# Adjacency build of a four-layer graph network: cells padded to one chunk of 128 edges in place of two

## The reference

```python
edge_index = jnp.stack([src, dst])
deg = jnp.maximum(jax.ops.segment_sum(jnp.ones(dst.shape, jnp.float32), dst, num_segments=1250), 1.0)
h = jnp.maximum(_layernorm(x, axis=-1), 0.0)
x = x + _L0_gnn_ref(h, src, dst, deg, ...)              # mean of neighbours
h = jnp.maximum(_layernorm(x, axis=-1), 0.0)
x = x + _L1_gnn_ref(h, edge_index, edge_weight, ...)    # two convolutions, weighted, normalised
h = jnp.maximum(_layernorm(x, axis=-1), 0.0)
x = x + _L2_gnn_ref(h, edge_index, edge_attr_128, ...)  # a message per edge, then a GRU
h = jnp.maximum(_layernorm(x, axis=-1), 0.0)
x = x + _L3_gnn_ref(h, edge_weight1, ..., src, dst)     # sum weighted by edge_weight1
```

## Time and profile before

| | |
|---|---|
| median of three runs | 1614.16 us |
| the profiled execution, its own time | 1613.28 us |
| its span | 1611.6 us |
| PE (TensorE) busy | 1336.9 us, 83% |
| DVE (VectorE) busy | 1173.5 us, 73% |
| POOL (GpSimd) busy | 798.6 us, 50% |
| ACT (ScalarE) busy | 620.8 us, 39% |
| mean granted TensorE clock | 0.948 |

### The profile page before, as it was taken

The page is one execution under the profiler, slowest core; times in us unless marked ns, Lnnn a source line. Parts: engine busy times, 40 slices in busy tenths (PEclk is TensorE's granted clock), DMA queues, the critical chain, the costliest instruction groups (busy, mean ns, idle before and its releaser), DMA issues.

```text
span 1611.6 us, 20246 instructions
## 1 busy us (share of the span) xinstructions
PE 1336.9 (83%) x4074; PEld 702.6 (44%) x4074; DVE 1173.5 (73%) x1917; ACT 620.8 (39%) x1580; POOL 798.6 (50%) x859
## 2 busy tenths in 40 slices
PE   0179169279999999896999888899899899999898
PEld 0144124134444444345875444444344444444665
DVE  8999863379999999982258277888888666666532
ACT  0122111066666662013001166777777422222310
POOL 1637777756666664677777256666666200000000
PEclk9989579689999999897999989999999999999999
DMA  8363402210000004444334476666566500000220
GB/s 347 108 263 120 117 22 80 87 32 0 0 0 0 0 0 190 152 134 154 101 92 127 170 223 218 186 186 178 171 187 190 142 0 0 0 0 1 78 86 31
DMA packets 81186, 168.21 MB, mean 104 GB/s; under 512 B 15436, under 2 KB 37838, under 8 KB 77812
## 3 DMA queue, kind: packets, MB, share of 16 engines
q1 hardware_dynamic: 52996, 102.58, 18.3%
q0 software_dynamic: 25472, 59.97, 13.3%
q10 hardware_dynamic: 2672, 5.11, 1.0%
HBM read 116.17 MB, written 51.44 MB: 104 GB/s over the span
## 4 chain that ended last, share of the span: by engine, by line
PE 52%; DVE 13%; DMA 12%; issue 11%; POOL 9%; ACT 2%; DVEq 0%; POOLq 0%; ACTq 0%; SPq 0%
PE pb L922 19%; PE pb L971 17%; POOL cell_rows L601 6%; DMA arena<-p_rows,gidx 5%; PE pb L998 5%; PE pb L1151 4%; DMA arena<-dst_rows 4%; DVE arena L1214 2%; DMA cell_rows<-pay,idx 2%; PE pb L1006 2%; POOL arena L662 2%; PE pb L908 1%; PE pb L1088 1%; DVE arena L1242 1%; DVE arena L1209 1%
## 5 line engine op out<-in xcount | busy, mean ns | idle before, releaser
L662 POOL DMA_INDIRECT arena<-p_rows,gidx x184 | 189.1, 1028 | 103.0 <-POOL gidx L658 72.8
L601 POOL DMA_INDIRECT cell_rows<-pay,idx x168 | 169.4, 1008 | 88.2 <-issue 46.6
L641 POOL DMA_INDIRECT dst_rows<-ering,idx x168 | 173.9, 1035 | 78.0 <-issue 37.1
L1088 PE MATMUL pb<-arena 128*128 128x512 f32 x368 | 197.0, 618 | 4.5 <-ACT arena L807 4.5
L971 PE MATMUL pb<-arena 128*128 128x384 f32 x368 | 141.2, 508 | 44.4 <-POOL arena L617 38.6
L1436 DVE TENSOR_TENSOR arena<-pb,arena 128x512 f32<-128x512 f32 x184 | 126.4, 687 | 66.4 <-DMA arena<-p_rows,gidx 61.0
L703 ACT ACTIVATE arena<-iota,cellm 128x128 f32<-128x128 f32 x368 | 127.7, 394 | 115.4 <-PE pb L971 78.4
L922 PE MATMUL pb<-ws,tiles 128*128 128x512 f32 (+1 forms) x360 | 147.3, 557 | 11.5 <-ACT tiles L674 11.5
L971 PE MATMUL pb<-tiles,arena 128*128 128x384 f32 x368 | 140.0, 504 | 6.0
L813 ACT ACTIVATE high<-arena 128x512 fp32r<-128x512 f32 x184 | 115.5, 627 | 75.6 <-DVE arena L1436 73.9
L1097 PE MATMUL pb<-high,low 128*128 128x512 f32 x184 | 111.4, 606 | 28.1 <-DVE low L1441 26.0
(11 more groups left out here) (205 smaller groups left out, 2227.7 us busy)
## 6 DMA issues: line engine op xcount, KB each, us to landing
dst_rows<-arena SPq DMA_DIRECT2D x6, 2046.0 KB, 18.1
arena<-dst_rows SPq DMA_DIRECT2D x46, 264.0 KB, 3.0
ering<-in_edge_attr_dram SPq DMA_DIRECT2D x41, 256.0 KB, 3.0
arena<-adj SPq DMA_DIRECT2D x10, 640.0 KB, 4.1
arena<-in_x_dram SPq DMA_DIRECT2D x18, 256.0 KB, 4.9
arena<-in_L_gnn_W_hh_dram SPq DMA_DIRECT2D x3, 1024.0 KB, 11.8
wt_hh<-ws SPq DMA_DIRECT2D x3, 1024.0 KB, 7.4
arena<-in_L_gnn_W_ih_dram SPq DMA_DIRECT2D x3, 1024.0 KB, 7.8
```

The source lines that it names most:

```text
L601: nc.gpsimd.indirect_dma_start(cell_rows[:, :], bass.IndirectOffsetOnAxis(idx1[:, c:c + 1], 0), pay1[:, c, :], None).then_inc(c_scattered[ ...
L641: nc.gpsimd.indirect_dma_start(dst_rows[:, :], bass.IndirectOffsetOnAxis(idx2[:, c + k:c + k + 1], 0), ering[:, 4 * q + k, :], None).then_ ...
L662: nc.gpsimd.indirect_dma_start(rows[:, k, :], None, p_rows[:, :], bass.IndirectOffsetOnAxis(gidx[:, k:k + 1], 0)).then_inc(g_landed[k], 16)
L1088: nc.tensor.matmul(e_bank(k)[:], erowT[:, k % 4], w1e_sb, start=True, stop=True).then_inc(edge_mm, 1)
```

## The change

Each cell is rounded up to whole chunks of 128 edges, not to whole pairs. There are then at most 272 chunks (34 turns of 8), and each is a step of its own on TensorE and VectorE: one product with `start` and `stop`, its own bank of the four, its own `block_done`, its own cell read from `cell_at` and its own add. Two adjacent chunks may now belong to different cells. The one-hots and their weights are still made for two chunks in one instruction, 136 times. A turn is now 8 chunks, four comparisons and eight adds, in the order comparison, add, add. The waits on the rings are counted in chunks: the one-hots' ring is as deep as before (8 chunks), the banks' ring now holds four chunks. The table of cells has three columns in `tabf` in place of two, and the destination table moves to the fourth; `cellm` becomes a part of a tile `free`, whose later users stay.

```diff
-CELL_PAIRS = (E + CELLS * (PAIR - 1)) // PAIR
-CELL_PAIRS = -(-CELL_PAIRS // 8) * 8
-CELL_CHUNKS = 2 * CELL_PAIRS
+CELL_CHUNKS = (E + CELLS * (P - 1)) // P
+CELL_CHUNKS = -(-CELL_CHUNKS // 8) * 8
...
-        cellm = sb("cellm", [P, CELL_CHUNKS, 4])
+        free = sb("free", [P, 2 * D + 2 * P])
+        cellm = free[:, 0:CELL_CHUNKS * 4].rearrange("p (c w) -> p c w", c=CELL_CHUNKS)
...
             def weights_turn(i):
-                for q in range(TURN):
-                    pool.wait_ge(dst_hot, TURN * i + q + 1)
+                for q in range(TURN // 2):
+                    pool.wait_ge(dst_hot, TURN // 2 * i + q + 1)
                     passed()
-                    hot = ohd(2 * (q % 4), 2)
+                    hot = ohd(2 * q, 2)
...
             def build_blocks():
                 def turn(i):
-                    for q in range(TURN):
-                        n, place = TURN * i + q, q % 4
-                        at_least(pe, block_added, n - 3)
-                        pe.wait_ge(src_hot, n + 1)
-                        pe.wait_ge(weighted, n + 1)
-                        for k in range(2):
-                            ins = nc.tensor.matmul(pb[place][:, 0:3 * P], ohs[:, 2 * place + k],
-                                                   ohd(2 * place + k, 1).rearrange("p a m d -> p (a m d)"), start=k == 0, stop=k == 1)
-                        ins.then_inc(block_done, 1)
+                    for k in range(TURN):
+                        at_least(pe, block_added, TURN * i + k - 3)
+                        if k % 2 == 0:
+                            pe.wait_ge(src_hot, TURN // 2 * i + k // 2 + 1)
+                            pe.wait_ge(weighted, TURN // 2 * i + k // 2 + 1)
+                        nc.tensor.matmul(pb[k % 4][:, 0:3 * P], ohs[:, k], ohd(k, 1).rearrange("p a m d -> p (a m d)"),
+                                         start=True, stop=True).then_inc(block_done, 1)
...
-            places(B1, cell_b, CELL_CHUNKS, "prefix1", idx1, [0, 1], THIRD, order_ready[0])
+            places(B1, cell_b, CELL_CHUNKS, P, "prefix1", idx1, [0, 1, 2], THIRD, order_ready[0])
...
             def hots(i, q):
 
-                n = TURN * i + q
-                at_least(dve, block_done, n - 3)
-                vtt(ohd(2 * (q % 4), 2)[:, :, 0], iota1[:].unsqueeze(1).to_broadcast([P, 2, P]),
-                    cellm[:, bass.ds(2 * TURN * i + 2 * q, 2), 1:2].to_broadcast([P, 2, P]), ALU.is_equal).then_inc(dst_hot, 1)
-
-            def add_block(i, q):
-
-                n = TURN * i + q
+                at_least(dve, block_done, TURN * i + 2 * q - 6)
+                vtt(ohd(2 * q, 2)[:, :, 0], iota1[:].unsqueeze(1).to_broadcast([P, 2, P]),
+                    cellm[:, bass.ds(TURN * i + 2 * q, 2), 1:2].to_broadcast([P, 2, P]), ALU.is_equal).then_inc(dst_hot, 1)
+
+            def add_block(i, k):
+
+                n = TURN * i + k
                 at = dve.value_load(cell_at[0:1, bass.ds(n, 1)], min_val=0, max_val=(CELLS - 1) * P)
                 dve.wait_ge(block_done, n + 1)
                 at_least(dve, block_added, n)
                 cell = matrices[:, :, bass.ds(at, P)]
-                vtt(cell, pb[q % 4][:, 0:3 * P].rearrange("p (m d) -> p m d", m=3), cell, ALU.add).then_inc(block_added, 1)
+                vtt(cell, pb[k % 4][:, 0:3 * P].rearrange("p (m d) -> p m d", m=3), cell, ALU.add).then_inc(block_added, 1)
 
             def turn(i, last):
-                for q in range(TURN):
-                    if not last or q < TURN - 3:
-                        hots(i + (q + 3) // TURN, (q + 3) % TURN)
-                    add_block(i, q)
+                for q in range(TURN // 2):
+                    if not last or q < TURN // 2 - 3:
+                        hots(i + (q + 3) // 4, (q + 3) % 4)
+                    add_block(i, 2 * q)
+                    add_block(i, 2 * q + 1)
```

More of the change, by code:

```diff
@@ L139, in build_gnn @@
         tabf = sb("tabf", [P, 4])
-        places_at = sb("places_at", [1, CELL_PAIRS + DST_PAIRS], I32)
-        cell_at = places_at[:, 0:CELL_PAIRS]
-        dst_at = places_at[:, CELL_PAIRS:]
+        places_at = sb("places_at", [1, CELL_CHUNKS + DST_PAIRS], I32)
+        cell_at = places_at[:, 0:CELL_CHUNKS]
+        dst_at = places_at[:, CELL_CHUNKS:]
         gidx = sb("gidx", [P, GROUP], I32)
@@ L240, in build_gnn @@
         w1e_sb = adj_part(D)
-        free = cellm[:].rearrange("p c w -> p (c w)")
         hot_far = free[:, 2 * D:2 * D + 2 * P].rearrange("p (c f) -> p c f", c=2)
@@ L453, in _ @@
                 sp.wait_ge(c_scattered[k], 16 * (J // COL))
-            sp.dma_start(cellm[:].rearrange("p c w -> p (c w)"),
+            sp.dma_start(free[:, 0:CELL_CHUNKS * 4],
                          cell_rows.rearrange("(p c) w -> p (c w)", p=P)[:, 0:CELL_CHUNKS * 4]).then_inc(cells_loaded, 16)
@@ L459, in _ @@
                 sp.dma_start(ering[:, 4 * q:4 * q + 4, 0:DE], edge_v[:, 4 * q:4 * q + 4, :]).then_inc(e_loaded[q], 16)
-            sp.wait_ge(block_added, CELL_PAIRS)
+            sp.wait_ge(block_added, CELL_CHUNKS)
             edges3 = [0, NT * D, (NT + 2 * KT) * D, 2 * NT * D, AW]
@@ L699, in turn @@
                 def turn(i):
[L700 to L701 removed]
+                    for q in range(TURN // 2):
+                        at_least(act, block_done, TURN * i + 2 * q - 6)
                         for k in (2 * q, 2 * q + 1):
[L703 to L704 removed]
+                            ins = nc.scalar.activation(ohs[:, k], iota1[:], ACT.Abs,
+                                                       bias=cellm[:, bass.ds(TURN * i + k, 1), 0:1].rearrange("p a w -> p (a w)"))
                         ins.then_inc(src_distance, 1)
[L706 to L707 removed]
+                        act.wait_ge(src_distance, TURN // 2 * i + q + 1)
+                        two = ohs[:, 2 * q:2 * q + 2].rearrange("p c s -> p (c s)")
                         nc.scalar.activation(two, two, ACT.Relu, bias=1.0, scale=-1.0).then_inc(src_hot, 1)
                 turn(0)
[L711 removed]
+                with act.Fori(1, CELL_CHUNKS // TURN) as i:
                     turn(i)
@@ L1017, in degrees @@
                 ins.then_inc(for_act, 1)
-            pe.wait_ge(block_added, CELL_PAIRS)
+            pe.wait_ge(block_added, CELL_CHUNKS)
             pe.wait_ge(z_loaded[0], 16)
@@ L1203, in _, with places @@
             link(vts(pay2[:, :, 1], dt_f, 1.0, -1.0, ALU.add, ALU.mult))
-            def places(buckets, bucket_of, chunks, job, idx, tab_cols, width, ready):
+            def places(buckets, bucket_of, chunks, unit, job, idx, tab_cols, width, ready):
                 ohb, csb = oh[:, 0:buckets], cs[:, 0:buckets]
@@ L1330, in add_block @@
                 cell = matrices[:, :, bass.ds(at, P)]
-                vtt(cell, pb[q % 4][:, 0:3 * P].rearrange("p (m d) -> p m d", m=3), cell, ALU.add).then_inc(block_added, 1)
+                vtt(cell, pb[k % 4][:, 0:3 * P].rearrange("p (m d) -> p m d", m=3), cell, ALU.add).then_inc(block_added, 1)
             def turn(i, last):
-                for q in range(TURN):
-                    if not last or q < TURN - 3:
-                        hots(i + (q + 3) // TURN, (q + 3) % TURN)
-                    add_block(i, q)
+                for q in range(TURN // 2):
+                    if not last or q < TURN // 2 - 3:
+                        hots(i + (q + 3) // 4, (q + 3) % 4)
+                    add_block(i, 2 * q)
+                    add_block(i, 2 * q + 1)
             dve.wait_ge(cells_loaded, 16)
             dve.wait_ge(wt_stored[0], 32)
-            turns = CELL_PAIRS // TURN
+            turns = CELL_CHUNKS // TURN
             for q in range(3):
@@ L1347, in _ @@
             turn(turns - 1, True)
-            dve.wait_ge(block_added, CELL_PAIRS)
+            dve.wait_ge(block_added, CELL_CHUNKS)
             def degree(m, t):
```

35 lines of the change are left out of this document (15 added, 20 removed).

## The result

The changed kernel takes 1637.68 us (median of 4 runs, 1636.04 to 1640.22) against 1613.74 us (4 runs, 1610.86 to 1614.77) on the same chip: a ratio of 1.0153, interval [1.0133, 1.0172]. It is 24 us slower. Its profiled execution took 1638.54 us with a span of 1636.8 us and a mean granted clock of 0.944, against 1613.28, 1611.6 and 0.948. A second comparison, among the experiments, gave 1.0129 [1.0097, 1.0161]. Ratios and their intervals leave out disturbed executions, which are slower at a lower granted clock; the medians of times in the experiments include them.

What follows compares the result with a forecast made beforehand. A comparison-weighting ring (VectorE, GpSimd) bound the build before; VectorE's queue would after: +19.8 (loop) - 1.1 (cell load) = +18.7 us on 1613.3, giving 1632, or 1633 by the median; range 1615 to 1655.

Steps and rivals of the forecast that it cites:

- the queue as the bound: Main forecast, chance 0.80: VectorE's in-order queue, 0.97 us an add, sets the changed build's pace at the high clock.
- Step 1, the ring alone: Build: the cycle comparison, GpSimd weighting, comparison, 1.597 us each, would alone give 217 us for 136 rounds, not 293.
- Step 2: Build: VectorE's queue needs 9.3 us a turn, so the loop ends at 644.1 us, +19.8 us.
- step 5: Before the build: loading fewer cells takes 3.2 us in place of 4.3, -1.1 us.
- Step 3: Build: a pair's second add waits for the first, 0.75 us start to start, covered by the queue's 0.97.
- Step 4: Build: four PSUM banks holding four chunks cost nothing; the comparison falls to 0.42 us without gain.
- VectorE's busy time down by over 100 us: Sign of the main forecast: VectorE's busy time falls by over 100 us while the loop is longer.
- Steps 5 and 6: Before the build: the shorter cell load, -1.1 us; the sort's extra table column, nothing, at most +0.5 us.
- Step 7: Behind the build: all engines wait for the last add and no operation changes, so the shift goes through whole.
- B: Rival, chance 0.08: the comparison and weighting cycle stays the build's bound, 217 us, about 1537 us in all.
- C: Rival, chance 0.07: TensorE's clock falls in the build; +37 us for half the time low, +73 for all.
- D: Rival, chance 0.05: an add costs only 0.85 to 0.91 us of queue; about no change, 1602 to 1617 us.

Runs made afterwards that it cites:

- 2: Changed kernel with the third matrix left out of the build: build 308.8 us, time 1852.63 us, ratio 1.011 to the kernel before.
- 1: Changed kernel with each add sent to a fixed cell, no place loaded in the build: build 216.9 us, time 1772.25 us, ratio 0.967.
- 4: Kernel before with the cell's place loaded twice for each add: build 346.3 us, time 1883.56 us, ratio 1.028.
- 6: Changed kernel without the run-time bounds check on the load of the cell's place: build 248.5 us, time 1785.2 us, ratio 0.980.
- 3: Kernel before with the third matrix left out of the build: build 225.8 us, time 1760.28 us, ratio 0.960.
- 5: Kernel before with each add sent to a fixed cell, no place loaded in the build: build 290.5 us, time 1850.86 against 1822.98 us.
- a_fixed: Same run as 1: changed kernel with adds to fixed cells, no place loaded in the build; 1772.25 us, ratio 0.967.
- a_unchecked: Same run as 6: changed kernel, the place's load without its run-time bounds check; 1785.2 us, ratio 0.980.
- after_again: Changed kernel run once more without an edit, beside the kernel before: 1635.43 us, ratio 1.0129.
- a_turn16: Changed kernel with turns of 16 chunks in place of 8: build 289.3 us, time 1607.9 us in its one run.
- a_unchecked_16: Changed kernel with the place's load unchecked and turns of 16 chunks: build 230.0 us, time 1553.08 us in its one run.
- a_unchecked_16_mid: Changed kernel with unchecked load, turns of 16 chunks and the comparison between a pair's two adds: build 224.5 us, time 1544.19 us, ratio 0.9558.
- a_two_matrices: Same run as 2: changed kernel, third matrix left out of the build; 1852.63 us, ratio 1.011.
- b_two_loads: Same run as 4: kernel before, the cell's place loaded twice for each add; 1883.56 us, ratio 1.028.
- four_per_load: Changed kernel with four chunks' places packed in one integer, loaded once for four adds: build 288.2 us, time 1826.3 us, ratio 1.005.

## Why the prediction was right, point by point

The predicted 1633 us stands against 1637.68, the shift of +18.7 against +23.9. (The loop's part of the sum is 644.1 - 624.4 = 19.7, not 19.8; it changes nothing.) The mechanism of the forecast, the queue as the bound, is shown: by 2 (the engines' work doesn't matter), 1, 4 and 6 (the queue's work does, both ways), 3 and 5 (in the kernel before it was the other way round).

- **Step 1, the ring alone.** 217 us for 136 rounds: a_fixed took 216.9.
- **Step 2, the turn.** 9.3 predicted, 9.23 measured; 32 turns 295.5 us (adds that start at 337.36 and 632.84) in place of 297.6, -2.1. The terms, too: 0.97 an add (three of four steps; the fourth is 0.90), 1.72 over the seam (0.97 + 0.17 + 0.58), and 0.28 in place of 0.25 for the comparisons' extra register operations. The last turn took 6.8 us (6.7), the first ended its last add's start at 337.4, where 339.2 less the earlier start of step 5 gives 338.1.
- **Step 3, the wait.** 0.75 us, hidden below 0.97. Uncovered in a_unchecked, it was 0.76.
- **Step 4, banks and comparison.** Nothing, and a mean of 0.43 us. But the sign "VectorE's busy time down by over 100 us" was too large: 1173.5 to 1082.9, -90.6 us. By the durations the comparisons lose 162 us (184 x 1.20 to 136 x 0.43) and the adds gain 51 (184 x 0.544 to 151.6), -111. But before, each add began inside the end of one comparison (472.07, and 470.94 + 1.21 = 472.15) and ended inside the start of the next, and busy time counts such a stretch once: some 28 us less to lose. After, adds and comparisons overlap by some 9 us. -111 + 28 - 9 = -92, against -90.6 measured: the overlap is what I left out.
- **Steps 5 and 6, the way to the build.** The first comparison came 2.1 us earlier, not 1.1. The load of the cells did take less (3.4 in place of 4.3 us from issue to landing, 0.9); the other 1.2 us are the scatter of the cells, which ended at 322.6 in place of 323.8 us. No reason for that was found in the change.
- **The end of the build.** 640.2 against 643.0: -0.7 by the start, -2.1 by the turns. +15.9 in place of +18.7.
- **Step 7, behind the build, is the step that failed.** "The shift goes through whole" gave 0, and the profiled execution shows +9.3 us. The build ended 2.8 us earlier than predicted, which hides a part of it in the sum; that is luck. From the end of the build to the end of the span it took 987.3 us before, 996.6 after, and 995.4 in after_again, which would fit a cost of the change. But the kernels with the same code and the same padding behind another build took 986.3 (a_turn16), 990.2 (a_unchecked_16) and 991.7 (a_unchecked_16_mid), one execution each, so that code and the padding alone don't bring it. Chance of one execution is unlikely too: the medians of the changed kernel are 24 and 22 us above the kernel before, and the build's end, where the profiles have it, accounts for 16 and 17 of them. One part was found, the low clock at the end of the build: the window of 37 us from there, before, after and in a_turn16 (us, PE busy (x), PEld, DVE, ACT, POOL, granted clock, DMA share, GB/s):

```profile
624.00:661.00 37.00, 36.61 (x100) 17.30 (x100) 36.91 (x18) 0.00 (x0) 12.03 (x16) 1.00 0.80 297
```

```profile
640.00:677.00 37.00, 36.77 (x89) 16.77 (x89) 36.73 (x18) 0.00 (x0) 10.52 (x14) 0.96 0.79 294
```

```profile
619.00:656.00 37.00, 36.19 (x97) 17.05 (x97) 36.71 (x18) 0.00 (x0) 11.16 (x15) 1.00 0.80 298
```

TensorE is as busy in all three, and gets 89 passes done where the others get 100 and 97. Its block of 80 passes takes 36.1 us in the changed kernel and 36.3 in after_again, and 34.6 to 34.7 in the kernel before and in a_turn16. That is 1.4 us on the chain. Most of the rest comes between the first load from `ys`, which starts 36.8 to 38.5 us behind the build in all the kernels compared, and the first gather: that starts 296.0 us behind the build before, 305.2 after, 303.4 in after_again, 301.7 in a_turn16 and 300.7 in a_unchecked_16_mid. In a_turn16 the end of the span doesn't come later for it: its first gather is 5.7 us late, and the time behind the build is 1 us shorter than in the kernel before. How the end of the build delays the gather, and when that reaches the end, stays open.
- **The rivals.** B (the ring stays) is false for the change and true of a_fixed. C (TensorE's clock falls in the build) didn't come: in the window from 460 to 490 us TensorE was busy 21.88 of 30 us (73%, where the prediction had 55 to 70%) at a granted clock of 1.00. As it happened, a_two_matrices ran its build at a mean of 0.73, and its turn was the same; with 256 columns a pass is shorter, so the prediction's price for 384 columns at the lower level stays untested. The price of C came in small, at the build's end, where I hadn't looked. D (an add at 0.85 to 0.91) was wrong by 0.06 to 0.12 us an add.
- **The Trainium skill** gives about 600 ns for a `tensor_load` (page "DMA: Bandwidth & Descriptors", section "Latency and other measured facts"); here 272 loads had a median of 303 ns, and the 80 us that the page's figure would have added did not come. The rule of "SBUF — State Buffer" ("Who interferes with whom") held again: with the comparison out of GpSimd's way its mean fell from 1.20 us to 0.44 and 0.41.

## What to carry to other kernels

Before a step is split into more, smaller ones, add up what each costs in its engine's own queue, register loads, checks, waits and loop seams, from the queue's records at the seam of a turn, where nothing waits. A busy share doesn't count any of that, and here it would have promised a gain of 76 us where 24 were lost. When the queue is the bound, take work out of the queue (the check of an address that is bounded anyway, every second seam) and put an independent instruction where one waits for the one before: together these three turned the same change into a gain of 70 us.

## What the runs showed of the hardware that was not expected

- The bounds check of a place loaded into a register costs 190 + 23 ns of VectorE's queue, more than two thirds of the load itself (303 ns); without it two adds went from 0.97 to 0.76 us apart.
- An add that waits for the previous one follows it by 0.75 us with a place from a register, by 0.65 with a fixed one (a_fixed), at the same 0.56 us of work. In four_per_load such adds came 0.83 to 0.93 us apart. The steps go with what lies in the queue between the record of the wait and the add: 0.07, 0.16 and 0.23 to 0.33 us. What is issued behind a wait is not hidden by it.
- A comparison in the ring with GpSimd may look short (0.55 us in a_fixed) with the ring unchanged: the wait that it shows depends on when it was issued, so a short duration is no proof that two engines don't exclude each other.
- In a window of 30 us in the build TensorE kept its high clock (granted 1.00) at 73% busy. At the end of the build the clock was granted low for 3.4 us, after 2.37 us without work, and in the kernel before, with 0.75 us at the same place, it wasn't. The idle time alone is not the cause: a_turn16 had 2.49 us there, b_two_loads 2.37, and both kept 1.00. What is stays open.
- In a_two_matrices the clock was granted low again and again during the build (mean 0.73, TensorE busy 223 of 296 us), though each pass had a third fewer columns than in the changed kernel, and the passes got no shorter on the whole. Less work for TensorE doesn't have to make its instructions shorter.
